# Cross-attention and a cosine/sine feed-forward on one core: V in one go, finer first loads, and phi's noise added on GpSimd

## The reference

```python
x = x + xattn(layernorm(x), ctx, mask)     # Q, K, V, Wo: 512x512 with biases, one head of 512
# scores = Q K^T / sqrt(512), masked, softmax over 77 keys, times V, times Wo
h = layernorm(x)
real = h @ cos(theta + theta_noise)        # 512x512
imag = h @ sin(phi + phi_noise)            # 512x512
x = x + sqrt(real*real + imag*imag)
```

## Time and profile before

| | us |
|---|---|
| median of 3 runs | 246.94 (246.16 to 250.35) |
| profiled execution, its own time | 245.63 |
| its span | 243.8 |
| TensorE busy | 236.7 |
| VectorE busy | 169.4 |
| ScalarE busy | 146.8 |
| GpSimd busy | 52.0 |

### The profile page before, as it was taken

One profiled execution on the slowest core, in us unless ns is written; L12 is line 12 of the kernel. 1 busy time (PEld: TensorE's weight loads), 2 busy tenths in 40 slices (PEclk: granted clock), 3 DMA queues, 4 the chain that ended last, 5 costly groups with the idle time before them and its releaser, 6 DMA issues.

```text
span 243.8 us, 3987 instructions
## 1 busy us (share of the span) xinstructions
PE 236.7 (97%) x1283; PEld 138.8 (57%) x1283; DVE 169.4 (69%) x339; ACT 146.8 (60%) x256; POOL 52.0 (21%) x154
## 2 busy tenths in 40 slices
PE   8999999999999999999999999999999999999992
PEld 2898656448544584458544854476447644444472
DVE  1674999897886966787668775877587753873443
ACT  2213398991498357944695378646873589266433
POOL 1002057210520332023302330033104310132000
PEclk9999999999999999999999999999999999999998
DMA  6999987965239825872487257744874326413622
GB/s 183 389 427 415 413 237 127 266 205 104 46 65 279 343 48 184 168 297 87 108 208 266 108 126 218 215 173 94 224 241 175 69 60 89 172 43 86 212 88 91
DMA packets 48525, 44.80 MB, mean 184 GB/s; under 512 B 42518, under 2 KB 42774, under 8 KB 45309
## 3 DMA queue, kind: packets, MB, share of 16 engines
q1 hardware_dynamic: 47557, 43.37, 57.5%
q0 software_dynamic: 288, 1.05, 2.6%
q10 hardware_dynamic: 664, 0.18, 0.3%
HBM read 25.66 MB, written 8.39 MB: 140 GB/s over the span
## 4 chain that ended last, share of the span: by engine, by line
PE 76%; DMA 8%; ACT 6%; DVE 5%; issue 2%; POOL 1%; SPq 1%; POOLq 0%; DVEq 0%; ACTq 0%
PE re L486 8%; PE re L488 7%; PE re L487 7%; PE im L486 7%; PE im L488 7%; PE im L487 7%; PE score_bank L536 7%; DMA wqT<-in_WqT 3%; DMA hT<-h_split 3%; PE att L464 2%; PE att L462 2%; DMA out_rows<-wv 2%; PE re L549 2%; PE im L549 2%; PE re L553 2%
## 5 line engine op out<-in xcount | busy, mean ns | idle before, releaser
L761 ACT ACTIVATE h<-x,shift,rstd 128x512 f32<-128x512 f32 x28 | 22.7, 809 | 32.9 <-POOL shift L369 32.8
L536 PEld LDWEIGHTS score_bank<-a_keys,xTb 128*128 128x128 f32 x192 | 35.9, 190 | 8.2
L486 PE MATMUL re<-w_hi,hT 128*128 128x512 f16 x100 | 37.9, 379 | 0.3 <-DMA hT<-h_split 0.3
L486 PE MATMUL im<-w_hi,hT 128*128 128x512 f16 x100 | 37.9, 379 | 0.0
L488 PE MATMUL re<-w_hi,hT 128*128 128x512 f16 x100 | 37.9, 379 | 0.0
L488 PE MATMUL im<-w_hi,hT 128*128 128x512 f16 x100 | 37.9, 379 | 0.0
L487 PE MATMUL re<-w_lo,hT 128*128 128x512 f16 x100 | 37.9, 379 | 0.0
L487 PE MATMUL im<-w_lo,hT 128*128 128x512 f16 x100 | 37.9, 379 | 0.0
L1042 DVE SCALAR_TENSOR_TENSOR h_split<-h,h_split 128x512 f16<-128x512 f32 x32 | 22.1, 691 | 21.2 <-ACT h_split L765 20.8
L536 PE MATMUL score_bank<-a_keys,xTb 128*128 128x77 f32 x192 | 32.8, 252 | 0.0
L780 ACT ACTIVATE sq_re<-re 128x512 f32<-128x512 f32 x27 | 15.8, 587 | 18.6 <-PE re L488 14.6
(11 more groups left out here) (178 smaller groups left out, 425.8 us busy)
## 6 DMA issues: line engine op xcount, KB each, us to landing
xTb<-in_xT SPq DMA_DIRECT2D x8, 1024.0 KB, 4.9
xb<-in_x SPq DMA_DIRECT2D x8, 1024.0 KB, 5.7
out_rows<-wv SPq DMA_DIRECT2D x7, 1024.0 KB, 4.2
wk<-in_Wk SPq DMA_DIRECT2D x2, 512.0 KB, 5.5
wqT<-in_WqT SPq DMA_DIRECT2D x4, 256.0 KB, 7.4
wv<-in_Wv SPq DMA_DIRECT2D x1, 1024.0 KB, 12.8
wo<-in_Wo SPq DMA_DIRECT2D x1, 1024.0 KB, 15.6
angle_w<-in_theta SPq DMA_DIRECT2D x2, 512.0 KB, 18.7
```

The lines of the kernel that those rows point to most:

```text
L486: nc.tensor.matmul(bank_[:, :], hT[j][:, 0, k, :], w_hi[part][:, k, :], start=(k == 0), stop=False)
L536: last = nc.tensor.matmul(score_bank[:, KEYS * j:KEYS * j + KEYS], xTb[:, k, P * j:P * j + P], a_keys[:, k, KEYS * batch:KEYS * batch + KEYS],
L761: nc.scalar.activation(h[j % 2][:, :], x2[b][:, j, :], ACT.Identity, bias=shift2[:, j:j + 1], scale=rstd2[:, j:j + 1]).then_inc(h_made, 1)
```

## The change

Four things change, all in the preparations and in group 0 and 1.

1. V^T is made for both batches at once: `values_of(c)` and `values_turned(c)` take all 154 columns, where they took 77 for each batch. ScalarE turns four slices, not eight.
2. Loads are finer: ctx in two halves, Wk in four chunks (K^T is now summed chunk by chunk, with the chunk loop outside), the second x in four tiles, theta and its noise in four quarters each, and these alternate with the tiles of x.
3. phi's noise is loaded plainly into its own buffer by the sync queue, and GpSimd adds it in two instructions of 1024 columns (`sum_phi`).
4. The hand-written orders on all five queues are adapted. The key norm matmul comes ahead of the first product, one `imag_and_score` block comes ahead of the sine's second half, and the load of xT for group 2 is issued between the transposes of tile 0 and of tile 1.

```diff
-            def load_angles(part, half):
+            def load_theta(c):
+                cols_ = slice(DIM * c, DIM * c + DIM)
+                sp.dma_start(angle_w[0][:, cols_], theta[:, cols_]).then_inc(ld_theta[c], 16)
+                sp.dma_start(angle_n[0][:, cols_], theta_noise[:, cols_]).then_inc(ld_theta[c], 16)
...
+            def load_phi_noise(half):
+                cols_ = slice(HALF * half, HALF * half + HALF)
+                sp.dma_start(angle_n[1][:, cols_], phi_noise[:, cols_]).then_inc(ld_phi[half], 16)
+
+            def load_second_x(j):
+                sp.dma_start(xb[1][:, j, :], x[1, 0, :, j, :]).then_inc(ld_second_x[j], 16)
...
             for half in range(2):
                 chunks = slice(CH // 2 * half, CH // 2 * half + CH // 2)
-                sp.dma_start(wk[:, chunks, :], Wk[:, chunks, :]).then_inc(ld_wk[half], 16)
+                sp.dma_start(ctx_t[:, chunks, :], ctxT[:, chunks, :]).then_inc(ld_ctx[half], 16)
+                for k in range(CH // 2 * half, CH // 2 * half + CH // 2):
+                    sp.dma_start(wk[:, k, :], Wk[:, k, :]).then_inc(ld_wk[k], 16)
...
-            load_x(1, 0)
-            load_angles(0, 0)
-            load_angles(0, 1)
-            load_angles(1, 0)
+            load_second_x(0)
+            load_second_x(1)
+            load_theta(0)
+            load_theta(1)
+            load_second_x(2)
+            load_second_x(3)
+            load_theta(2)
+            load_theta(3)
+            load_phi(0)
+            load_phi_noise(0)
             sp.wait_ge(scores_mm, 1)
             load_xT(1, 0)
-            load_angles(1, 1)
+            load_phi(1)
+            load_phi_noise(1)
...
-            transpose_h(0, [0, 1])
+            transpose_h(0, [0])
             sp.wait_ge(scores_mm, 2)
             load_xT(0, 1)
+            transpose_h(0, [1])
             transpose_h(0, [2])
...
-                pool.dma_start(angle_w[1][:, cols_], phi_noise[:, cols_], accum_op=ALU.add).then_inc(phi_summed[half], 16)
+                nc.gpsimd.tensor_tensor(angle_w[1][:, cols_], angle_w[1][:, cols_], angle_n[1][:, cols_],
+                                        ALU.add).then_inc(phi_summed[half], 1)
...
-            def values_of(b, c):
+            def values_of(c):
 
                 bank_ = prep[2 + c] if c < 2 else prep[4 + c]
-                cols_ = slice(KEYS * b, KEYS * b + KEYS)
                 for k in range(CH):
-                    last = nc.tensor.matmul(bank_[:, cols_], wv[:, k, P * c:P * c + P], ctx_t[:, k, cols_],
+                    last = nc.tensor.matmul(bank_[:, 0:KK], wv[:, k, P * c:P * c + P], ctx_t[:, k, :],
                                             start=(k == 0), stop=(k == CH - 1))
...
+            pe.wait_ge(key_norm_made, 1)
+            nc.tensor.matmul(pT_bank[:, 0:1], ones_keys[:, :], key_norm[:, :], start=True, stop=True).then_inc(vw_norm_mm, 1)
             feed_first(0, 0, 0)
             feed_first(0, 0, 1)
-            pe.wait_ge(key_norm_made, 1)
-            nc.tensor.matmul(pT_bank[:, 0:1], ones_keys[:, :], key_norm[:, :], start=True, stop=True).then_inc(vw_norm_mm, 1)
             feed_first(1, 0, 0)
             feed_first(1, 0, 1)
             feed_first(0, 1, 0)
             feed_first(2, 0, 0)
+            imag_and_score(1, 0, 0)
             feed_first(0, 1, 1)
             feed_first(2, 0, 1)
-            imag_and_score(1, 0, 0)
-            imag_and_score(1, 1, CH)
+            imag_and_score(1, 1, 4)
```

282 lines of the change are left out of this document (140 added, 142 removed).

## The result

| | before | after |
|---|---|---|
| median of 4 runs | 247.02 us (246.16 to 250.35) | 256.11 us (255.75 to 256.52) |
| profiled execution, its own time | 245.63 | 255.75 |
| span | 243.8 | 253.8 |
| mean granted clock of TensorE | 0.996 | 0.978 |

What follows compares the result with a forecast made beforehand. TensorE's queue was taken to set the end, level with the first tile's transposition. Second tile at 47.0 us gave +0.2: 245.6 + 0.2 = 245.8 profiled, with the median 1.3 above, 247.1 us; range 244.6 to 249.6.

Steps and rivals of the forecast that it cites:

- new waits of TensorE after 60 us: Sign of a wrong prediction: TensorE waiting anew beyond 60 us, past the first products.
- From there all products, scores and the PE work stand in a sequence of the same length: After the second tile's product starts (set at 47.0 us), the remaining sequence was taken as unchanged, giving +0.2 us.
- TensorE idle for 2 to 4 us in all: Sign of a right prediction: TensorE idle ahead of the products or second tile, waiting for VectorE's sine or a transposing DMA.
- are covered by that room: New TensorE waits for the first group's vw cost some tenths, covered by being ready 3.3 us before 44.01.
- I cost it at nothing: Key part in quarters ends tenths sooner, but matmuls wait for WqT's centring, issued three DMAs later: -0.2 to +0.3.
- More DMAs, each issued in about 0.45 us, keep well ahead of that: Finer loads' issues stay ahead of transfers; last theta quarter lands at 29.3 us, phi's noise at 31.9.
- The chain on VectorE: VectorE's passes from 29.4 us to the sine's low half: ready at 41.8 undisturbed, 44.4 us with GpSimd holding it.
- the hold: GpSimd's second addition, right ahead of the second tile's low half, holds that VectorE pass 2.3 us; products start at 44.5.
- GpSimd's additions: Two 128x1024 additions of phi's noise on GpSimd, taken as 2.3 us each, possibly up to 4.6.
- The tie: GpSimd's first addition (31.9 us) against VectorE's second reduction (31.85); VectorE first forecast; rival GpSimd wins: +2.4 us, chance 0.22.
- The second brake: Second tile's transposition queued behind the 1 MB xT load; that tile's product starts between 46.2 and 47.1 us.
- TensorE's own work: Wide V matmuls remove 2.6 us, turned-values wait 0.6; TensorE ready for products at 40.7 us, gaining at most 3.3.

Runs made afterwards that it cites:

- V alone: Kernel before with only V made for both batches at once, and the TensorE and ScalarE order that goes with it; 248.06 us, ratio 1.005.
- the larger pieces: Changed kernel with ctx loaded whole and Wk in halves, as before; 255.19 us, ratio 1.034.
- the version with four edits: Changed kernel with VectorE's order put back, both transposes ahead of the xT load, ctx and Wk in larger loads, 18 products of zeros; 248.06 us, ratio 1.006.
- the norm-first version: The addition on VectorE, with the norm's read and last tile's residual and statistics moved ahead of the sine's low half and phi's second sum; 247.72 us, ratio 1.006.
- the sine's low halves first with zeros: The norm-first version with the sine's first low half ahead of the last residual and statistics, its second ahead of phi's sum, 14 zeros; 248.84 us, ratio 1.010.
- the addition on VectorE: The version with four edits, but phi's second sum made by VectorE instead of GpSimd, and 14 products of zeros; 249.63 us, ratio 1.012.
- the last pair of runs: The norm-first version with the sine's low halves moved earlier, with 14 products of zeros and without; 248.84 and 248.72 us, both ratio 1.010.

## Why the prediction was wrong

The forecast was 247.1 us, with a chance of 0.05 for "slower". Measured were 256.1. Of the signs named for being wrong, "new waits of TensorE after 60 us" is the one that came.

1. "From there all products, scores and the PE work stand in a sequence of the same length": wrong, and the largest miss. TensorE's sequence was the same, VectorE's was not. The diff moves two calls ahead of two others behind group 1, and I had followed VectorE's order only to the low halves of the sine. Putting them back gives 5.9 us, and 250.2 us for the kernel, still 3 us over the forecast.

2. TensorE standing still was priced at nothing. I expected "TensorE idle for 2 to 4 us in all" ahead of the products, wrote that new waits "are covered by that room", and put no term for the clock behind such a wait into the sum. The runs show a price: 2.3 us behind the 3.9 us wait, 1.9 behind the 3.3 us one. V alone makes the kernel 0.5% slower (1.002 to 1.009); there the clock is one part of the loss, and not shown to be all of it. The page TensorE: Matmul & The Clock Gate of the Trainium skill (Wait — 56ns, not 53.3ns?) gives 426.7 ns for a step of 512 columns at the lower of the two clocks and 215.7 at the upper; the trace agrees, with 0.43 and 0.216 us.

3. "I cost it at nothing" for WqT (-0.2 to +0.3), and "More DMAs, each issued in about 0.45 us, keep well ahead of that": mis-sized. The first matmul with centred WqT came at 12.19 us, and at 11.04 with the larger pieces; in the time this was 0.9 us. Theta's last quarter was there at 31.0, not 29.3 us, and phi's noise at 34.3, not 31.9. In the fifth slice of the page the loads moved 362 GB/s, where they had moved 413 and I had reckoned 415. The table above ties this to the finer pieces: the 1.7 us are the bytes that were missing by 30 us. The sync queue's issues also back up (2.26 us for one at 10.90 us, 4.26 for the two at 13.21). By what the finer pieces slow the transfers is open, and between executions of the same loads theta's last sum moved by over 1 us (30.81 to 31.96).

4. The chain on VectorE was right, with the hold in it. From the last theta sum to the end of the sine's low half I had 44.4 - 29.4 = 15.0 us; it took 45.89 - 31.00 = 14.9. It merely began 1.6 us later, and with it the products (46.04 against 44.5).

5. GpSimd's additions, 2.3 us each: the first took 2.52, the second 2.96, both begun inside a pass of VectorE; in the version with one of them it took 2.36. The estimate of 2.25 us from the GPSIMD Engine Reference of the Trainium skill (Performance versus the Vector engine) is a little under all of them.

6. The hold: right in place and size, 2.15 us where I took 2.3. It is confirmed from both sides, by its going away without the addition (0.68 us) and by its presence in the version with four edits (2.85). The page SBUF — State Buffer of the Trainium skill (Who interferes with whom) holds here in both directions: the low half waited for the addition, and the inverse norm for VectorE's passes. In the second direction the inverse norm's time was once that of one pass (1.46 us) and once that of four (4.33 us), beside the same passes.

7. The tie was won by VectorE, as forecast, and with 0.9 us to spare (33.41 against 34.33), since phi's noise was later than theta.

8. The second brake is real: with the products at full clock the second tile was waited for 0.98 us. The forecast had it landed by 46 us; its transposition was issued at 44.4 and took 5.5 us. In the change itself this was hidden behind the slow products.

TensorE's own work was sized right: V alone freed it at 40.3 us, where I had 40.7. The loss I had bounded by the hold alone, and it lay in two other things: a fall of the clock, which the profile of before does not have, and an order behind the part that I had followed, which the diff does show.

## What to carry to other kernels

Where TensorE is the bound, work taken from it in front of a wait is worth nothing, and can be worth less than nothing if it turns the cover into a pause: V alone lost 0.5% while doing less. First shorten what it waits for. A hand-written order has to be compared to its last row on every engine, not up to the first place of interest, since one pair of calls in the wrong order cost more than everything else in this change. And a long GpSimd instruction should stand beside VectorE operations with one input in SBUF, and GpSimd's small ones too where something waits for them.

## What the runs showed of the hardware

- TensorE's granted clock fell to half behind waits of 3.9, 3.3 and 4.1 us, and it fell behind four shorter ones as well: 2.06 us, 1.81 us, 1.84 us in the changed kernel with x and theta in larger pieces, and 2.02 us in the norm-first version with them. It did not fall behind one of 0.98 us, nor behind 1.58 and 1.94 us (the sine's low halves first with zeros, and the addition on VectorE). So the length of the wait alone does not decide. In the change it was back at 51.5 and 95.9 us, when TensorE had been at work again for 5.5 and 4.1 us. Products of zeros in the gap kept it up.
- GpSimd's power of one column took 0.55 us beside a residual and statistics, and 1.46 or 4.33 us beside two-input passes of VectorE. The 4.33 us ended only with the fourth pass in a row; beside the same four passes it took 1.46 us in six other runs, the changed kernel among them.
- Loads of x and theta in pieces of 256 KB, where 512 KB or more stood before, went with a lower rate in their stretch: 392 against 415 GB/s from 18 to 30 us, and 415 again with the larger pieces of x and theta.
- The clock of a gap is not always lost time: where a later limit follows within some microseconds, as in the last pair of runs, it is taken back there.
